# Last chunk's down products in two steps per tile, ended tile by tile, and a new order by offsets for single groups of instructions

## The reference

```
x = x + 0.5 * ffn(layernorm(x))
x = x + attn(layernorm(x))          # 16 heads of 16, rotary q and k, causal, softmax
x = x + 0.5 * ffn(layernorm(x))
ffn(x): (silu(x @ gate_w.T * gate_s) * (x @ up_w.T * up_s)) @ down_w.T * down_s   # 256 -> 704 -> 256
```

## Time and profile before

| | |
|---|---|
| median of 3 runs (lowest to highest) | 816.71 us (815.28 to 823.77) |
| the profiled execution, and its span | 817.89 us, 816.2 us |
| PE busy | 785.5 us (96%) |
| DVE, ACT, POOL busy | 618.3, 547.6, 389.9 us (76, 67, 48%) |
| mean granted clock of TensorE | 0.99 |
| fillers (L900) | 142 matmul records, 27.4 us |

### The profile page before, as it was taken

How to read it: one execution, slowest core, us unless ns; L and a number is a source line. 1 busy time by engine, 2 the same in 40 slices (tenths; PEclk the granted TensorE clock), 3 DMA queues, 4 the chain that set the end, 5 groups by cost and what they waited for, 6 DMA issues and landing times.

```text
span 816.2 us, 17340 instructions
## 1 busy us (share of the span) xinstructions
PE 785.5 (96%) x6160; PEld 529.5 (65%) x6160; DVE 618.3 (76%) x1263; ACT 547.6 (67%) x1064; POOL 389.9 (48%) x430
## 2 busy tenths in 40 slices
PE   5999999999999999999999999999999999999995
PEld 4788878767555555565554575554556447888985
DVE  5676577899898998898988888998889725555442
ACT  3765665533786877757767857777787896566542
POOL 2777768533444552263461253331232445665553
PEclk8999999999999999999999999999999999999998
DMA  9900252502463766273555454652662112010011
GB/s 307 353 2 1 78 155 78 157 1 53 123 196 99 192 186 170 73 192 117 170 120 144 107 120 140 165 122 74 186 121 57 44 41 65 16 39 27 27 39 41
DMA packets 65795, 89.78 MB, mean 110 GB/s; under 512 B 19756, under 2 KB 31404, under 8 KB 65452
## 3 DMA queue, kind: packets, MB, share of 16 engines
q1 hardware_dynamic: 65564, 88.57, 38.3%
q10 hardware_dynamic: 144, 0.07, 0.0%
HBM read 45.52 MB, written 40.76 MB: 106 GB/s over the span
## 4 chain that ended last, share of the span: by engine, by line
PE 83%; ACT 6%; DVE 4%; issue 3%; POOL 1%; DMA 1%; SPq 0%; POOLq 0%; DVEq 0%; ACTq 0%
PE psum L922 17%; PE psum L1027 16%; PE psum L1010 12%; PE psum L890 12%; PE psum L985 10%; PE psum L948 10%; ACT PT L1135 3%; PE psum L995 3%; PE psum L908 2%; DVE NP L1256 2%; PE psum L900 1%; POOL HL_f L1316 1%; DMA RD<-wd 1%; DVE HH_f L1216 1%; ACT HH_f L1099 1%
## 5 line engine op out<-in xcount | busy, mean ns | idle before, releaser
L1135 ACT ACTIVATE PT<-psum 128x512 f32<-128x512 f32 (+2 forms) x640 | 309.9, 583 | 105.7 <-PE psum L1010 103.9
L1256 DVE TENSOR_REDUCE NP<-psum 128x1 f32<-128x512 f32 (+2 forms) x448 | 261.0, 644 | 25.6 <-PE psum L995 17.2
L1367 POOL TENSOR_SCALAR_AFFINE_SELECT PT<-PT 128x512 f32<-128x512 f32 x128 | 80.2, 636 | 177.3 <-ACT PT L1135 170.8
L1010 PE MATMUL psum<-Q,K 50*128 50x512 f32 (+2 forms) x768 | 143.9, 409 | 3.4 <-ACT PT L1135 0.9
L922 PE MATMUL psum<-XH,WG_f 128*128 128x512 f32 x352 | 143.7, 408 | 2.4 <-issue 2.0
L985 PE MATMUL psum<-K,Q 48*128 48x512 f32 (+2 forms) x768 | 140.5, 392 | 3.7 <-ACT PT L1135 2.5
L1027 PE MATMUL psum<-PT,V 128*32 128x512 f32 (+3 forms) x1536 | 143.8, 492 | 0.1
L922 PE MATMUL psum<-XL,WG_f 128*128 128x512 f32 x352 | 139.4, 396 | 0.0
L1316 POOL TENSOR_TENSOR HL_f<-HF_f,HH_f 128x512 fp32r<-128x512 f32 x80 | 103.2, 1296 | 71.4 <-ACT HH_f L1099 71.4
L1010 PEld LDWEIGHTS psum<-Q,K 50*128 50x128 f32 x768 | 67.9, 184 | 76.7 <-issue 27.9
L1209 DVE SCALAR_TENSOR_TENSOR HF_f<-psum,US,G_f 128x512 f32<-128x512 f32 x90 | 67.3, 750 | 58.8 <-ACT G_f L1088 31.7
(11 more groups left out here) (83 smaller groups left out, 1053.5 us busy)
## 6 DMA issues: line engine op xcount, KB each, us to landing
zd<-ZH SPq DMA_DIRECT2D x32, 512.0 KB, 3.9
Q<-zd SPq DMA_DIRECT2D x64, 192.0 KB, 3.8
K<-zd SPq DMA_DIRECT2D x64, 192.0 KB, 4.8
zd<-ZL SPq DMA_DIRECT2D x16, 512.0 KB, 4.8
od<-OS SPq DMA_DIRECT2D x32, 256.0 KB, 3.0
OC<-od SPq DMA_DIRECT2D x32, 128.0 KB, 2.7
SC<-rd_ SPq DMA_DIRECT2D x32, 128.0 KB, 2.8
out<-X SPq DMA_DIRECT2D x16, 256.0 KB, 2.1
```

The costliest lines, as they stand in the source:

```text
L1010: ins = tn.matmul(dst, K[k][r, p, j * P:(j + 1) * P], Q[k][r, p, 512 * c2 + base:512 * c2 + 512], start=True, stop=True)
L1135: sc.activation(dst, src, ACT.Exp, scale=0.25).then_inc(S["act_exp"], 1)
L1256: ve.tensor_reduce(out=acc, in_=src, axis=AX, op=ALU.max, negate=True).then_inc(S["dve_max"], 1)
L1367: gp_.affine_select(out=pt, in_=pt, compare_op=ALU.is_ge, fill=0.0, base=0, pattern=[[0, 4], [1, P]], channel_multiplier=-1).then_inc(S["p ...
```

## The change

Two things. First, the last chunk of the second FFN alone (`by_tile`) gets its down products in two steps per tile: pe_da with the 8 matmuls of blocks 0 to 3 (DOWN_FIRST = 4), which waits only for those, and pe_dn with the 3 of blocks 4 and 5. Each tile has a PSUM bank of its own, and each is ended alone: dve_t2 of 256 columns, the addition to X by POOL for the first pair (pool_x) and by DVE for the second (dve_xe), and a store of 128 KB.

Second, the planner's numbers are others (MODE_PLACE, LOAD_PLACE, FORMS, WARM_SHARE, WINDOW, URGE, PACE), the row passes (normalise, transpose, q/k/v) are entered in a written order (PASSES), and a table NUDGE adds an offset to the place of single groups of pieces. Which instructions there are stays the same but for the last chunk and the fillers (71 pieces before, 63 now); their order changes on all engines.

```diff
-MODE_PLACE, DMA_RATE, WINDOW = 1.604, 200.0, 63.692
+MODE_PLACE, DMA_RATE, WINDOW = 2.94, 200.0, 107.2
-RELOAD_NS, LOAD_PLACE = 115, 1.0
+RELOAD_NS, LOAD_PLACE = 115, 8.2
-FORMS = {"full": 1.0, "col": 0.681, "mask": -0.176, "half": -0.019}
+FORMS = {"full": 7.4, "half": 0.2, "mask": -0.01, "col": 11.5}
-        self.place[piece], self.ns[piece], self.after[piece] = place, ns, [x for x in after if x]
+        self.place[piece], self.ns[piece], self.after[piece] = place + nudged(piece), ns, [x for x in after if x]
...
+NUDGE = {
+    "rows": {("a", 1): -48, ("a", 3): -16, ("a", 5): -32, ("f1", 1): -26, ("f1", 5): 4, ("f1", 6): -36, ("f1", 7): -69, ("f2", 0): -31,
...
+def nudged(piece):
+
+    kind, a = piece[0], piece[1:]
+    if kind in FAMILY:
+        family = FAMILY[kind]
+        two = (a[0], a[1] // 4) if family == "s" else a[0:2]
+        own = None if kind in ("pe_s", "pe_st") else a[0:3] if family == "qkv" and kind not in ("pe_v", "act_v") else two
+        return NUDGE.get(family, {}).get(two, 0) + (NUDGE.get(kind, {}).get(own, 0) if own else 0)
...
+        for pr, tt in ((pr, tt) for pr in range(2) for tt in range(2) if by_tile(ph, c)):
+            key = at + PACE["down"][0] + PACE["down"][1] + pr + 0.5 * tt
+            add(key - 3, 960, "pe_da", ph, c, pr, tt, after=last[:2 * DOWN_FIRST] + w, room=(1,))
+            add(key, 360, "pe_dn", ph, c, pr, tt, after=last + [("pe_da", ph, c, pr, tt)], room=("with", ("pe_da", ph, c, pr, tt)))
...
+            add(key + 2, dve_ns(256) + 100, "dve_t2", ph, c, pr, tt, after=[("pe_dn", ph, c, pr, tt), ("pool_x",) + t2],
+                empties=[("pe_da", ph, c, pr, tt)])
+            add(key + 2, dve_ns(256) if pr else pool_ns(256), "dve_xe" if pr else "pool_x", ph, c, pr, tt, after=[("dve_t2", ph, c, pr, tt)])
+            add(key + 2, 600, "dma_out", c, pr, tt, after=[("dve_xe" if pr else "pool_x", ph, c, pr, tt)], size=1.3e5)
```

More of the change, by code:

```diff
@@ L331 @@
 QUOTA = {"pe_s": 5, "pe_st": 5}
[L334 to L337 removed]
+PACE = {"ffn 1": np.float64(17.449), "ffn 2": 16.4, "heads": np.float64(27.849), "first heads": np.float64(36.242),
+        "ffn 2 after heads": np.float64(-23.291),
+        "first q, k, v": (np.float64(74.083), np.float64(149.891), np.float64(72.672), np.float64(171.675)),
+        "q, k, v": (np.float64(0.454), 1.35, np.float64(2.451)), "rows ahead": np.float64(5.305),
+        "first maxima": (132.395, np.float64(77.935), np.float64(175.181)), "maxima": np.float64(1.498), "pv": np.float64(-0.217),
+        "projection": (np.float64(23.482), np.float64(6.998)), "rows": (2.396, np.float64(7.651), np.float64(1.704)),
+        "column block": np.float64(3.384), "down": (np.float64(12.494), 6.708)}
@@ L340, in x_ready @@
+PASSES = ([("f1", c) for c in range(4)] + [("a", 0), ("f1", 4), ("f1", 5), ("a", 1), ("f1", 6), ("f1", 7)] + [("a", c) for c in range(2, 2 * B)]
+          + [("f2", c) for c in range(8)])
 def x_ready(who, c):
@@ L929, in tensor_program @@
                     tn.matmul(bank(*piece)[0:1, 0:6], ONE, FL[:, 8:14], start=True, stop=True).then_inc(S["pe_flag"], 1)
-                elif kind == "pe_dn":
+                elif kind in ("pe_da", "pe_dn"):
                     ph, c, pr, tt = a
-                    if tt == 0:
+                    split = by_tile(ph, c)
+                    some = range(NI) if not split else range(DOWN_FIRST) if kind == "pe_da" else range(DOWN_FIRST, NI)
+                    if kind == "pe_da" if split else tt == 0:
                         take(piece)
-                    dst, rows = bank(*piece)[:, tt * D:(tt + 1) * D], slice((2 * pr + tt) * P, (2 * pr + tt + 1) * P)
+                    off = 0 if split else tt * D
+                    dst, rows = bank(*piece)[:, off:off + D], slice((2 * pr + tt) * P, (2 * pr + tt + 1) * P)
                     terms = []
-                    for i in range(NI):
+                    for i in some:
                         s = slot[f"hf{ph}", (ph, c, i)]
@@ L947, in tensor_program @@
                         h, w = part[:, rows], WD[ph][:, i, :]
-                        ins = tn.matmul(dst, f32(h) if general else h, f32(w) if general else w, start=(n == 0), stop=(n == len(terms) - 1))
-                    ins.then_inc(S["pe_dn"], 1)
+                        ins = tn.matmul(dst, f32(h) if general else h, f32(w) if general else w, start=(n == 0 and some[0] == 0),
+                                        stop=(n == len(terms) - 1 and some[-1] == NI - 1))
+                    ins.then_inc(S[kind], 1)
                 elif kind == "pe_qk":
```

99 lines of the change are left out of this document (80 added, 19 removed), and 6 rows, old and new, of the table NUDGE.

## The result

The changed kernel took **795.77 us** (median of 4 runs, 795.06 to 797.5), the kernel before 816.0 measured beside it (4 runs, 814.82 to 823.77): a ratio of **0.974, 95% interval 0.970 to 0.978**. The profiled execution took 795.64 us with a span of 793.7, 22.5 less than the span of before; the 2.3 us beyond the 20.2 lie in which two executions were profiled (817.89 us and 795.64). The kernel before, measured again beside the experiments, had medians of 816.56, 818.72 and 818.17, so a difference of 1 to 3 us between the times of two kernels from different groups of runs is not clear of noise; the ratio to the before measured beside them is the better guide.

A forecast was written before the change was run, and what follows sets the result against it. TensorE was taken as the bound, VectorE close behind. Terms -5.8 (end), -2.9 (waits inside the FFNs), -2.8 (attention order) and +0.8 (shape changes) gave -10.7, so 806.0 us; 8-in-10 range 798 to 814.

The forecast's parts named there:

- part 1: Last chunk of the second FFN: down products start earlier and the way out is shorter, 5.8 us less.
- Rival B: Last chunk: the clock stays at the lower level, so the split gains only 1.8 us; 810.0 us in all, chance 0.07.
- Part 2 (a): First chunk of the first FFN: correction ahead of GpSimd's rounding, six fillers gone, transposes earlier; 1.0 us less.
- Part 2 (b): Chunk 4: VectorE's correction stands before a pair of rotation products, so TensorE's idle time goes; 1.1 us less.
- (c): Second FFN, chunk 2: one more piece of work fills the idle time before 723.02; 0.8 us less.
- Part 3: Attention: 28 fewer PSUM bank reuses that wait, at 0.1 us each, 2.8 us less; changes of shape cost 0.8 more.
- sign-post: New profile: waits of score loads were to be 38 us or less instead of 43.7.
- 0.8 us more for changes of shape: TensorE, whole kernel: 603 changes of matmul shape instead of 582, 18 of the 21 at 0.02 us and 3 at 0.15.
- Rival C: Attention: bank reuses are worth their ceiling; 18.8 us less in all, 798 us, chance 0.16.
- Rival D: Attention: VectorE becomes the bound and score products wait for it; slower, up to 836 us, chance 0.06.

The follow-up runs named there:

- the two runs with 44 extra products: The changed kernel with 44 unread products ahead of gate/up products in chunks 3 to 6 of the second FFN: 806.99 us over 128 rows, 823.94 us over 64.
- the run with the fillers there: The kernel before with the last chunk split and more filler products at the start and ahead of the first FFN's last down products: 810.25 us.
- the two regrouped orders: TensorE's order alone changed: six pieces of the step in the kernel before with split and extra fillers, 811.0 us; 30 pieces in the changed kernel, 802.2 us.

## Why the prediction was right in sign and too small

**The end (part 1, -5.8): right.** The down products have 0.66 us idle ahead of them for the forecast's less than 1, stand 0.12 us apart at the full clock, and the two short operations took 0.42 and 0.43. The stage is 5.8 us shorter. Rival B fell: no clock near 0.5 in the down products. Four stores in place of two cost nothing that shows, as the earlier trace rows had it: the span ends 3.8 us after the last addition, 3.7 before. The Trainium skill's advice to coalesce ("DMA: Bandwidth & Descriptors", "Rules for kernel authors") is for small transfers and names 64 KB as the size below which one pays mostly overhead; these stores of 128 KB lie above it, so this run doesn't speak against the rule. What the prediction did not say is that in the new order, too, the old end idles 1.85 us and loses the clock, fillers and all, so that the split is also what keeps it.

**Part 2 (a), -1.0: the step that failed first.** It priced one wait and a few fillers and did not look at the clock of the start, which was at 0.51 from 17 to 22 us. It forecast 1.0 us for the start, and the traces show 4.7. The rows of the first chunk now (answers to the earlier trace rows):

```profile
27.63 2.53 POOL L1413 TENSOR_TENSOR HL_f<-HF_f,HH_f 128x512 fp32r<-128x512 f32 x2 [0.48 <-ACT HH_f L1182]
...
32.81 3.55 POOL L1408 TENSOR_TENSOR WQL<-RQ,WQH 128x1536 fp32r<-128x1536 f32 x1
```
```profile
32.48 0.60 PE L987 MATMUL psum<-IDT,XN 128*128 128x128 f32 x4
33.15 0.35 PE L1030 MATMUL psum<-WD_f,HH_f 128*128 128x256 f32 x1
```

The mechanism was right (the corrections are ready by 30.16, the weights' part comes behind). "The down products can't start much before 36.5" was wrong: they start at 33.15. Of the stage's 4.7 us some 2.4 are clock and 2.3 the order. The clock's part is in one trace of seven of that order, so it is in part luck; in six of them the stage gained 2.3 to 4.0. Before, six filler pieces ended at 12.63 and TensorE idled until 14.45. Now there are seven, at the lower clock themselves, so they last until the flag's product. (That doesn't keep the clock for certain: in the two runs with 44 extra products they last as long, and the level is down again from 16.7.)

```profile
11.87 2.59 PE L979 MATMUL psum<-IDT 128*128 128x128 f32 x14
14.39 0.19 PE L1008 MATMUL psum<-FL,CST 128*1 128x6 f32 x2
```

**Part 2 (b), -1.1 and (c), -0.8.** (b) came: 79.5 to 77.9, so -1.6. But its cause is only half told. In the kernel before, VectorE's correction of chunk 4 took 1.81 us, because GpSimd worked on a correction of its own beside it:

```profile
114.64 1.81 DVE L1216 TENSOR_TENSOR HH_f<-HF_f,HH_f 64x512 fp32r<-64x512 f32 x1
```
```profile
114.62 1.28 POOL L1316 TENSOR_TENSOR HL_f<-HF_f,HH_f 128x512 fp32r<-128x512 f32 x1 [2.31 <-ACT HH_f L1099]
```

Without that the same operation takes 0.69 us, and so it does in this chunk of the kernel after. With 0.69 it would have ended at 115.33 and not at 116.45, behind the rotation as it stood; the down products would have waited for GpSimd's correction of block 4 alone, until 115.90, half as long. So about half of the 1.13 us comes from the two corrections meeting; no run moved one of them by itself. (c) came too, but the stage around it gained 3.8, by waits (7.6 to 4.0) and changes of shape (4.3 to 3.3) as the count of the traces has it: 3.0 us for which the prediction had no term. No run takes these apart.

**Part 3, -2.8 + 0.8.** For the attention itself this was the right size: -1.6. Its sign-post was wrong, though: the waits of score loads were to fall to 38 us and rose to 48.9. The waits that count, those of the pieces that really start late, fell by 2.5 us by the count above, and by about 1 if a piece's usual time is taken for each pair of neighbours. A wait of a load lies in part beside the product ahead of it, so that table can rise while the lateness falls.

The **0.8 us more for changes of shape** was the other step that failed. It was a sum over the kernel (582 to 603), and most were held to be free. The price is 0.37 to 0.39 us for a pair, and place decides: in the step to the attention 40 became 29 and 6.8 us became 3.4. At the measured price eleven changes make 2.1 us; the other 1.3 of that column no run has priced. With the 1.2 us of clock, 0.5 of waits and 0.3 of fillers that makes 4.1 of the step's 5.2 us, for which the prediction had no term, and the run with the fillers there shows that 4.0 of them are not clock. A count by stage, which the same orders give, would have shown the sign.

So the sum failed in three terms: the start (4.7 for 1.0), the step (5.2 for 0) and the attention's end (3.8 for 0.8) make 11.9 us more than forecast, and the spans differ from the forecast by 11.8.

Rival C's 798 came nearest, but not for its reason: the reuses of banks were not worth their ceiling. Rival D named the true danger of reordering. It did not happen here, and the two regrouped orders ran into waits of that kind.

**What stays open.** Whether the lower level reaches the first gate products in most executions of the kernel after, as in six of the seven traces of that order. Whether a regrouping of the step with VectorE's order changed as well would keep the 2.1 us of changes: I moved TensorE's pieces only. Which of the start's 2.3 us of order belong to the wait (1.1) and which to fillers (1.1) is only the count of the trace. And the waits of the attention's end are shown to come with the offsets behind 431 us, but not which of them.

## To carry to other kernels

Where a matmul engine is full, count changes of matmul shape by stage, not over the kernel, and price each at what the trace shows for one in and one out; alternating two shapes piece by piece is the costly pattern. Don't regroup on one engine alone: in both orders that I regrouped so, the saving came back as a wait for the engine that empties the banks. And look at the granted clock of the first products and of those behind every idle piece before pricing anything there: filler products ahead of them were worth some 2 us at the start and 1.2 in the step, but those ahead of the old end did not keep the clock.

## What I had not expected of the hardware

- The lower clock level comes at different times in executions of the same order. In seven kernels whose TensorE order is the same until the first down products, a stretch at 0.5 began at 10.3 us (the kernel after), 18.8, 16.2, 16.8, 15.2, and in two at 9.9 and again at 16.7; the first stage took 32.2 to 34.6 us. Nor does the level fall at once: behind the 1.85 us of idle time without the split, the down products ran at the full clock for 1.5 us first (788.70 to 790.2). A single profile can mistake this for an effect of 2 us.
- A filler over all rows between two gate products costs 0.23 us, against 0.13 in a row of fillers, and 0.09 of it falls on the step behind the filler.
- VectorE's correction and GpSimd's work slow each other. Alone the correction took 0.68 to 0.69 us in every trace. Where a GpSimd operation of 512 columns or more was under way when it began, it took 1.08 us with 0.53 of them together (785.10, the last chunk of the kernel after), 1.23 with 0.68 and 1.49 with 0.94 (both without offsets), 1.81 with 1.26 (114.64, before): each time 0.55 us plus the time together. (In one chunk of the second FFN it was less: 0.93 with 0.62 before, 0.89 with 0.49 after.) Beside GpSimd's operations of 4 columns it took 0.69. The one that starts second seems to pay: VectorE's addition to X took 0.43 us where it began 0.04 us before one of GpSimd's, which then took 0.98 for 0.73 (the kernel after), and 0.79 where it began 0.21 us behind one (the split alone). VectorE's maxima and rotations, which read PSUM, took 0.68 with and without GpSimd at work.
